# The order in which an attention block's 16 query-key products are issued on TensorE

## The reference, cut to what matters

```python
xn = _layernorm(x)
q = _rmsnorm((xn @ wq.T).reshape(B, L, 16, 64));  k = _rmsnorm((xn @ wk.T).reshape(B, L, 4, 64))
v = (xn @ wv.T).reshape(B, L, 4, 64)           # k, v: 4 heads, repeated to 16
attn = jnp.einsum('bqhd,bkhd->bhqk', q, k) * scale + bias   # -inf outside a window of 17 keys
out  = jnp.einsum('bhqk,bkhd->bqhd', softmax(attn), v) @ wo.T
r = sigmoid(xr @ W_r.T);  ffn = r * (square(relu(xk @ W_k.T)) @ W_v.T)   # xr, xk mix x with its predecessor
y = x + out + ffn
```

## Time and profile before

| | us |
|---|---|
| median of the runs before (2 runs, 2027.57 to 2038.5) | 2033.03 |
| the profiled execution | 2047.56 |
| its span, from first to last instruction, core 5 | 2046.0 |
| TensorE matmul busy in it (88%) | 1808.1 |
| VectorE busy (24%) | 498.6 |
| ScalarE busy (9%) | 189.0 |
| GpSimd busy (3%) | 53.2 |

### The profile page before, as it was taken

How to read it: one execution, slowest core, us unless ns; L and a number is a source line. 1 busy time by engine, 2 the same in 40 slices (tenths; PEclk the granted TensorE clock), 3 DMA queues, 4 the chain that set the end, 5 groups by cost and what they waited for, 6 DMA issues and landing times.

```text
span 2046.0 us, 17394 instructions; the slowest of 8 cores (2007.0 to 2046.0 us)
## 1 busy us (share of the span) xinstructions
PE 1808.1 (88%) x7264; PEld 1091.1 (53%) x7264; DVE 498.6 (24%) x610; ACT 189.0 (9%) x260; POOL 53.2 (3%) x36
## 2 busy tenths in 40 slices
PE   2798789999799889999979968899997996889998
PEld 0443589644253379954426338884442532888443
DVE  0344332000342333101044233300004423330010
ACT  0001111000000111100000011100000001110000
POOL 0000000001100000000110000000011000000001
PEclk9898699899899667789989968968898996896999
DMA  7021000422312000032231200013023120001311
GB/s 212 1 82 41 1 1 1 125 82 82 123 42 82 0 1 1 1 125 82 82 123 41 82 0 1 1 55 129 23 82 123 41 82 0 1 1 47 118 41 41
DMA packets 59844, 112.81 MB, mean 55 GB/s; under 512 B 1860, under 2 KB 10312, under 8 KB 59544
## 3 DMA queue, kind: packets, MB, share of 16 engines
q1 hardware_dynamic: 59768, 111.70, 17.0%
HBM read 103.31 MB, written 8.39 MB: 55 GB/s over the span
## 4 chain that ended last, share of the span: by engine, by line
PE 84%; DVE 7%; ACT 4%; issue 3%; DMA 1%; DVEq 1%; SPq 1%; POOL 0%; ACTq 0%; POOLq 0%
PE psS L176 29%; PE psA L176 28%; PE psB L176 24%; DVE pbuf L176 2%; PE psPV L176 2%; DVE lrow L176 1%; DVE xnbuf L176 1%; ACT ptbuf L176 1%; DMA xbuf<-xin 1%; DVEq L176 1%; ACT asub L176 1%; ACT pbuf L176 1%; SPq L176 1%; ACT L176 1%; DVE lbuf L176 1%
## 5 line engine op out<-in xcount | busy, mean ns | idle before, releaser
L176 PE MATMUL psS<-xmix,wslot 128*128 128x512 f32 x512 | 235.9, 621 | 0.0
L176 PE MATMUL psA<-asub,wslot 128*128 128x112 f32 (+1 forms) x1280 | 194.2, 316 | 33.6 <-ACT asub L176 32.7
L176 PEld LDWEIGHTS psA<-asub,wslot 128*128 128x128 f32 x1280 | 185.3, 230 | 37.7 <-issue 37.6
L176 PE MATMUL psB<-asub,wslot 128*128 128x112 f32 (+1 forms) x1280 | 194.1, 317 | 0.0
L176 PEld LDWEIGHTS psB<-asub,wslot 128*128 128x128 f32 x1280 | 187.8, 233 | 0.0
L176 PEld LDWEIGHTS psS<-xmix,wslot 128*128 128x128 f32 x512 | 101.9, 200 | 128.9 <-issue 128.9
L176 PE MATMUL psA<-xnbuf,wslot 128*128 128x512 f32 x256 | 125.4, 638 | 12.8 <-DVE xnbuf L176 10.1
L176 PE MATMUL psA<-xmix,wslot 128*128 128x512 f32 x256 | 124.0, 641 | 10.1 <-ACT xmix L176 7.8
L176 PE MATMUL psS<-scr,wslot 128*128 128x512 f32 x256 | 117.3, 619 | 0.0
L176 PE MATMUL psB<-xmix,wslot 128*128 128x512 f32 x256 | 114.4, 600 | 0.3 <-DMA wslot<-w_wr 0.3
L176 PE MATMUL psS<-xnbuf,wslot 128*128 128x512 f32 x256 | 111.2, 592 | 0.0
(11 more groups left out here) (95 smaller groups left out, 1456.5 us busy)
## 6 DMA issues: line engine op xcount, KB each, us to landing
wslot<-w_wq SPq DMA_DIRECT2D x8, 2048.0 KB, 14.7
wslot<-w_wo SPq DMA_DIRECT2D x8, 2048.0 KB, 9.0
wslot<-w_wr SPq DMA_DIRECT2D x8, 2048.0 KB, 8.3
wslot<-w_wkf SPq DMA_DIRECT2D x8, 2048.0 KB, 13.6
wslot<-w_wvf SPq DMA_DIRECT2D x8, 2048.0 KB, 12.0
xbuf<-xin SPq DMA_DIRECT2D x4, 2112.0 KB, 19.3
yout<-xnbuf SPq DMA_DIRECT2D x4, 2048.0 KB, 9.7
wslot<-w_wk SPq DMA_DIRECT2D x4, 1024.0 KB, 12.9
```

Source lines behind the costliest of these rows:

```text
L176: inst = getattr(eng, attr)(*a, **kw)
```

## The change

In `emit_qk` the loop that issued slots 0, 1, 2, ... 15 now issues 0, 8, 1, 9, 2, 10, ... 7, 15. Everything computed from s in the body (the head, the partitions, the columns of qbuf, kbuf and psS) is as it was.

```diff
@@ -651,7 +651,8 @@
                     T.wait_ge(psS_free[0], psS_free[1])
                     mm_gate("S0")
                     mm_gate("S1")
-                for s in range(NH):
+                for j in range(NH):
+                    s = (j // 2) + 8 * (j % 2)
                     h = 2 * (s % 8) + s // 8
                     pq = 64 * (h % 2)
                     ciq = h // 2
```

## The result

The changed kernel is faster: 1988.52 us median (11 runs, 1975.5 to 2033.65) against 2036.7 (10 runs, 2016.16 to 2051.04). That is 44 us, with an interval from 34 to 54; the forecast of 32 lies just under it. The interval of the ratio has the 2% bound inside it, so the runs do not say on which side of it the gain lies.

A forecast was written before the change was run, and what follows sets the result against it. The prediction took TensorE's chain, with QK on it, as the bound. Overlapping row halves saved 23.0 us in three attention stages and 9.4 in the second, about 32, clock nothing: 2033 - 32 = 2001 us, range 1978 to 2022.

The forecast's parts named there:

- 2% bound: Whole kernel: about 2%, 41 us, is what a measurement can tell from no change.
- What bounds: TensorE holds 84% of the chain that ended last; QK, 79.31 us busy, is on the path and shortening it counts.
- The step that could not be read off: QK calls: overlap seen over about three records of each half taken for sixteen; 1.38 us less per full-clock call.
- The term that I mis-sized: Clock effects in PV and projections: nothing added; gains up to 3 and 8 us, or about 8 us lost.
- The bound of 3 us in the PVs of subtile 1: PV of subtile 1: an earlier clock return gains at most 0.8 us each, 3 us in all.
- the evacuation behind the softmax: Projections of subtiles 2 and 3: VectorE's evacuation keeps about 0.8 of at most 2.9 us clock gain each.
- the 8 that I had as their bound: Projections of subtiles 2 and 3: some 2 us less half-clock loss in perhaps four of eight, 8 us.
- The drain at each change of half: Rival in QK: each change of row half costs 0.09 us and nothing overlaps; 2067 us, chance 0.04.
- Weight loads: Rival in QK: both halves' loads share one path, 3.0 us a call against 3.38; 2025 us, chance 0.09.
- The engine's look-ahead: Rival in QK: only a far later matmul is let in, so the reorder does nothing; 2033 us, chance 0.05.
- The rival with the clock's gain: QK's 32 us plus 3 in PV and 8 in the projections from the clock; 1990 us, chance 0.10.

The follow-up runs named there:

- the blocks of four: QK's slots issued 0-3, 8-11, 4-7, 12-15 instead of the sequential order of the kernel before; ratio 0.989, interval 0.975 to 1.003.

## Why the prediction was right, point by point

**What bounds.** TensorE's chain, and in it QK wherever it stands. Right: the waits behind QK kept their length, 11.06 in subtile 0, 2.74 in 2, 1.25 in 4, and all of QK's loss arrived. Only in subtile 1 the wait for asub grew, from 1.25 to 1.83 us, and that came from PV.

**The overlap.** The step that could not be read off, three overlapping records standing for sixteen, held fully. Predicted per call 1.38, 2.67 and 0.86 us less; measured 3.38 - 2.00 = 1.38, 6.42 - 3.76 = 2.66, and 0.85 in the narrow subtile (2.17 to 1.32). On undisturbed cores 4 x 7.67 = 30.7 us were due and 30.6 came (34.1 on core 1). "How late does the second half start" was the right thing to ask of the old trace.

**The sum.** 32 us were forecast for the core of the profile, whose second tile ran at a lowered clock and so had more to lose; on a core without that it is 31. The whole gain was 37 us there and 44 (34 to 54) in the timed runs. The term that I mis-sized is the clock, which I had put at nothing between plus 11 and minus 8. Inside attention it was plus 4 to 8 on cores 0 to 3, and after what the rest of the kernel gave and took, 5 us of the 37 are not QK's. The bound of 3 us in the PVs of subtile 1 held for PV (2.6 to 2.7), and the run with the new order in subtile 1 alone shows that this part belongs to QK itself. But it should have been nought: the evacuation behind the softmax, which I subtracted in subtiles 2 and 3, stands in subtile 1 too and took all of it back (83.8 us for PV and projection in both kernels). What arrived instead is 1.2 to 1.8 us in the last PV of the tiles, which I hadn't looked at, and 2.9 to 6.2 us in the projections of subtiles 2 and 3, inside the 8 that I had as their bound. These fell differently from tile to tile and core to core, and no run ties them to a cause: that they came out as a gain and not as a loss is luck.

**The rivals.** The drain at each change of half is refuted by the call times, though its price is real: 0.09 us is also what an entry cost in the blocks of four, once for each time that a half had run empty. The rule of the Trainium skill ("TensorEngine Tiling (Array Packing)", Key Properties) named in the prediction, that changing the tile alone doesn't drain, agrees with 15 changes in 2.00 us. Weight loads do not bind: 32 loads fit into the same 2.00 us, 0.06 each. The engine's look-ahead is about three waiting records on a half, enough for strict alternation. The rival with the clock's gain came closest to what happened, at about half of its size (5 of 11 us) and without its term in PV.

**The wait that I had not weighed** is the one that made the same edit fail in PV: I looked for where a shorter QK would only lengthen a wait, found none, and that is what separates the two.

## What to carry to other kernels

Matmuls that use half of the rows or half of the columns took six tenths of the time (3.38 to 2.00 us, 2.95 to 1.75) once those of the other half stood close behind them in program order, with up to four records of one half in a row and neighbours of different halves in different banks, as here; no work is saved, so look at the order first. Before doing it, find what ends the wait behind the group: with nothing in between the whole gain arrives, with another engine's work there it becomes idle time of TensorE, and 3.9 us of it here went with a lowered clock in what followed. Follow it past the first wait too: what PV gained in subtile 1 passed the copy and was lost two groups later, at an evacuation. Then move the work that waits, here one copy ahead of one exponential, with two more banks for the projection, and the same edit pays.

## What the runs showed of the hardware

- Two row halves, and two column halves, each kept the pace of one alone at full clock: 0.109 us a record for QK, 0.096 for PV, over 16 records each side by side. The other half gets in when three records of the running half are left waiting (QK in the old order at 1.38 us, PV at 1.21). In QK, entering a half that has run empty costs 0.09 us more than the pace (0.200 to the second start, where the pace is 0.109).
- QK on one half at half clock, 6.4 us with no gap, left the clock at half; on both halves, 3.8 us long, it was followed by a PV of 3.1 to 4.0 us, shorter than the 4.9 to 5.5 of before. The rows show the order of events, not what the clock goes by.
- A granted clock of 0.81 fell on some cores of a die and not on others in the same execution: in that of before, cores 4 and 5 spent 231 and 228 us at it and had spans of 2044.9 and 2046.0 us, cores 6 and 7 of the same die spent none and had 2009.4 and 2013.4 us. The Trainium skill ("TensorE: Matmul & The Clock Gate", Part 1) describes a limit of 13/16 for the whole die; here it held pairs of cores.
